# Joining the layer-2 experts, their combination and the layer-3 linear attention into one program per engine, with the keys computed in step with the queries

## The reference

```python
# layer 2, feed-forward: top 2 of 8 experts, then layer norm
h = gelu(einsum('bsd,edf->bsef', x, w1) + b1)
expert_out = einsum('bsef,efd->bsed', h, w2) + b2
out = einsum('bse,bsed->bsd', gate_probs, expert_out)      # 2 rows per token
out = (out - mean) / sqrt(var + 1e-5) * ln_g + ln_b
x = x + tanh(g_ffn[2]) * out
# layer 3, linear attention (8 heads of 64)
q = softmax(layer_norm(layernorm(x) @ Wq, ln_q_g, ln_q_b), -1) * 8
k, v = split(context @ Wkv); k, v = with a null key and value in front
k = softmax(k, over tokens)
ctx = einsum('bhnd,bhne->bhde', k, v)
out = layer_norm(einsum('bhnd,bhde->bhne', q, ctx)) @ Wout
x = x + tanh(g_xattn[3]) * out
# layer 3, feed-forward: top 2 of 8 experts with a capacity
```

## Time and profile before

| | |
|---|---|
| median of 3 runs | 1698.0 us (1695.79 to 1702.94) |
| the profiled execution | 1712.41 us, its span 1710.7 us |
| mean granted TensorE clock | 0.865 |
| busy over the span: PE, DVE, ACT, POOL | 71%, 58%, 40%, 47% |
| layer-2 experts, first weight load to last store | 831.0 to 1015.0 us |
| combination, first load to last instruction | 1023.7 to 1085.2 us |
| linear attention, first load to last scatter | 1085.9 to 1424.3 us |
| layer-3 experts and last combination | 1432.4 us to the end |

### The profile page before, as it was taken

The page is one execution under the profiler, slowest core; times in us unless marked ns, Lnnn a source line. Parts: engine busy times, 40 slices in busy tenths (PEclk is TensorE's granted clock), DMA queues, the critical chain, the costliest instruction groups (busy, mean ns, idle before and its releaser), DMA issues. The chain is left out here.

```text
span 1710.7 us, 36170 instructions
## 1 busy us (share of the span) xinstructions
PE 1217.5 (71%) x11764; PEld 981.9 (57%) x11764; DVE 992.1 (58%) x2935; ACT 691.6 (40%) x1614; POOL 812.3 (47%) x1064
## 2 busy tenths in 40 slices
PE   3888864918888697554489960388888853999991
PEld 2666653916676474344378850256666643888881
DVE  3877861247998575576122219678888841444444
ACT  2766641316887253442133320145555421222222
POOL 1347564517776135456344430145777762333334
PEclk9998976967999798775699985699999976999996
DMA  5322203633331002011466633100000002222215
GB/s 131 104 90 88 71 14 101 199 78 125 107 112 52 13 2 67 8 39 46 135 194 191 195 104 99 38 2 2 15 18 18 18 26 75 63 77 61 75 38 152
DMA packets 156107, 130.03 MB, mean 76 GB/s; under 512 B 21402, under 2 KB 133804, under 8 KB 155952
## 3 DMA queue, kind: packets, MB, share of 16 engines
q1 hardware_dynamic: 144688, 106.98, 22.0%
q0 software_dynamic: 11264, 21.07, 3.6%
...
## 5 line engine op out<-in xcount | busy, mean ns | idle before, releaser
L1324 POOL DMA_INDIRECT l_rows_out<-l3e_y,l3e_target x80 | 77.8, 973 | 176.0 <-DVE l3e_y L1311 163.8
L1278 ACT ACTIVATE l3e_sT<-l3e_ps_h 128x256 f32<-128x256 f32 x160 | 61.5, 384 | 177.9 <-PE l3e_ps_h L1248 151.5
L1324 POOL DMA_INDIRECT l_rows_out<-l2e_y,l2e_target x80 | 77.8, 972 | 115.0 <-DVE l2e_y L1309 97.2
L1297 DVE TENSOR_TENSOR l3e_hT<-l3e_sT,l3e_ps_h 128x256 f32<-128x256 f32 x160 | 67.4, 421 | 99.5 <-ACT l3e_sT L1278 97.9
L1275 ACT ACTIVATE l2e_hT<-l2e_ps_h,l2e_b 128x256 f32<-128x256 f32 x160 | 66.9, 474 | 111.5 <-PE l2e_ps_h L1243 101.7
L1247 PE MATMUL l3e_ps_h<-l3e_xT,l3e_w 128*128 128x256 f32 x320 | 101.0, 398 | 4.9 <-DVE l3e_xT L1288 0.6
L1248 PE MATMUL l3e_ps_h<-l3e_xT,l3e_w 128*128 128x256 f32 x320 | 96.6, 384 | 0.0
L1040 POOL DMA_INDIRECT l_rows_in<-l2a_rt_rows,l2f_slot x64 | 62.9, 982 | 61.0 <-DVE l2f_slot L1030 43.6
L1257 PE MATMUL l2e_ps_y<-l2e_w,l2e_hT 128*128 128x128 f32 x640 | 81.3, 281 | 1.0 <-issue 0.9
L1257 PEld LDWEIGHTS l2e_ps_y<-l2e_w,l2e_hT 128*128 128x128 f32 x640 | 77.0, 196 | 2.2 <-issue 1.8
L1243 PE MATMUL l2e_ps_h<-l2e_xT,l2e_w 128*128 128x256 f32 x320 | 77.6, 386 | 0.7 <-DVE l2e_xT L1288 0.6
...
## 6 DMA issues: line engine op xcount, KB each, us to landing
...
```

Of the source, the lines that this page charges most:

```text
L1278: nc.scalar.activation(sT[:, f % 2, :], ps_h[f % 2][:, 0:CHUNK], act_func).then_inc(s_ready, 1)
L1297: nc.vector.tensor_tensor(hT[:, b, f, :], sT[:, f % 2, :], ps_h[2 + f % 2][:, 0:CHUNK], ALU.mult).then_inc(h_ready, 1)
L1324: pool.indirect_dma_start(out=r.rows_out, out_offset=bass.IndirectOffsetOnAxis(ap=target[:, c % 2, a:a + 1], axis=0), in_=y[:, c % 2, a, : ...
```

## The change

The three phases become one, `experts_then_attention`: no barrier between them, and each engine runs the experts' part, then the linear attention's. `Combine` is no longer a phase; its parts stand inside the linear attention's steps, four tiles at a time, and are spread over ScalarE (weighting `scale`, normalising `normal`), GpSimd (`total`, `root`, `update`) and VectorE (moments, `offset`). The loop now begins at step -17 instead of -6. Since x is turned raw and not normalised, the layer norm in front of the queries goes into the weights (centred columns, `wqc`, `wq_total`) and into the variance (`x_eps_of`); ScalarE's L2226 and the shared `statistics` of the phase fall away. The null key's exponent is its own small ScalarE instruction instead of a VectorE addition (L2336). SyncE issues the gains and the attention's weights ahead of the experts' loads, and VectorE adds the shift to x ahead of the experts. KEY_LEAD = 0 and KEY_EARLY = 0 mean that the keys of tile i+3 stay in step i, as before. The diff, cut to its core:

```diff
+KEY_LEAD = 0
+KEY_EARLY = 0
...
+    def scale(self, act, t):
+        if not self.is_tile(t):
+            return
+        if t % 4 == 0:
+            act.wait_ge(self.arrived[t // 4], 32)
+        for k in (1, 0):
+            self.nc.scalar.activation(self.got[:, k, t, :], self.got[:, k, t, :], ACT.Copy, scale=self.r.weight[:, k, t:t + 1]
+                                      ).then_inc(self.s["scaled"], 1)
+
+    def total(self, pool, q):
+        if not self.is_quad(q):
+            return
+        at = slice(4 * q, 4 * q + 4)
+        pool.wait_ge(self.s["scaled"], 8 * q + 8)
...
+    def root(self, pool, q):
+        if not self.is_quad(q):
+            return
+        at, s = slice(4 * q, 4 * q + 4), self.s
+        pool.wait_ge(s["mom_ready"], 4 * q + 4)
+        pool.wait_ge(s["filled"], 1)
+        pool.tensor_scalar(self.veps[:, q % 2, :], self.moments[:, at, 1], LN_EPS, None, ALU.add).then_inc(s["veps_ready"], 1)
+        pool.wait_ge(s["veps_ready"], q + 1)
+        pool.tensor_tensor(self.rstd[:, at], self.veps[:, q % 2, :], self.half[:, :], ALU.pow).then_inc(s["root_ready"], 1)
+
+    def offset(self, dve, q):
+        if not self.is_quad(q):
+            return
+        at = slice(4 * q, 4 * q + 4)
+        dve.wait_ge(self.s["root_ready"], q + 1)
+        self.nc.vector.scalar_tensor_tensor(out=self.nmr[:, at], in0=self.moments[:, at, 0], scalar=-1.0, in1=self.rstd[:, at],
+                                            op0=ALU.mult, op1=ALU.mult).then_inc(self.s["nmr_ready"], 1)
...
+        act.wait_ge(self.s["nmr_ready"], t // 4 + 1)
+        self.nc.scalar.activation(self.got[:, 0, t, :], self.got[:, 0, t, :], ACT.Identity, scale=self.rstd[:, t:t + 1], bias=self.nmr[:, t:t + 1]
+                                  ).then_inc(self.s["normed"], 1)
...
+        at, s = slice(4 * q, 4 * q + 4), self.s
+        pool.wait_ge(s["gated"], 2)
+        pool.wait_ge(s["shifted"], 1)
+        pool.wait_ge(s["normed"], 4 * q + 4)
+        got = self.got[:, 0, at, :]
+        pool.tensor_tensor(got, got, self.lnp[:, 0, :].unsqueeze(1).broadcast_to([P, 4, D]), ALU.mult).then_inc(s["gained"], 1)
+        pool.wait_ge(s["gained"], q + 1)
+        pool.tensor_tensor(self.core.x[:, at, :], self.core.x[:, at, :], got, ALU.add).then_inc(s["added"], 1)
...
+            pool.wait_ge(s["xnT_ps"], t + 1)
+            pool.wait_ge(s["qsq_ready"], t + 1)
+            pool.wait_ge(before.s["xbn_ready"], t + 1)
+            pool.tensor_tensor(core.x[:, t, :], core.x[:, t, :], shift[:, :], ALU.add).then_inc(s["x_shifted"], 1)
...
+        for i in range(FIRST, NT + 9):
+            query_centred(i + 2)
+            key_norm(key_tile(i) - 2)
+            router.prefix(pool, quad(i - 5))
+            router.scatter_tile(pool, i - 9)
+            roots(i)
+            before.update(pool, quad(i + 9))
+            shifted(i + 3)
+            null_values(key_tile(i))
+            router.roots_on_pool(pool, quad(i - 1))
+            before.root(pool, quad(i + 13))
+            before.total(pool, quad(i + 17))
+        router.scattered(pool)
...
+            pe.wait_ge(before.s["added"], t // 4 + 1)
+            reused(pe, s["qb_ready"], t - 1)
+            nc.tensor.transpose(ps_x, core.x[:, t, :], core.ident[:, :]).then_inc(s["xnT_ps"], 1)
...
+        for i in range(FIRST, NT + 9):
+            k = key_tile(i)
+            turned_keys(k - 1)
+            query_exponents(i + 1)
+            before.normal(act, i + 9)
+            turned_outputs(i - 1)
+            key_exponents(k)
+            turned_queries(i + 1)
+            values(k)
+            before.scale(act, i + 17)
+            turned_x(i + 5)
+            router.turned(act, quad(i - 3), ps_t)
+            router.normalise(act, quad(i - 2))
...
+        for i in range(FIRST, NT + 9):
+            k = key_tile(i)
+            query_maximum(i + 2)
+            before.offset(dve, quad(i + 12))
+            query_squares(i + 4)
+            query_denominators(i)
+            query_variance(i + 4)
+            outputs(i)
+            key_maximum(k)
+            output_moments(i)
+            key_centred(k)
+            output_mean(i)
+            query_offset(i + 3)
+            output_variance(i)
+            combined(k - 1)
+            before.row_moments(dve, i + 13)
+            residual(i - 1)
+            before.x_moments_of(dve, i + 5)
+            before.row_mean(dve, i + 13)
+            router.read(dve, quad(i - 4), ps_l)
+            router.slots(dve, quad(i - 5), ps_l)
+            key_denominators(k - 1)
+            before.x_mean_of(dve, i + 5)
+            summed(i - 1)
+            before.x_eps_of(dve, i + 5)
+            router.choose(dve, quad(i - 4))
+            router.aggregate(dve, i - 1, s["summed"])
+            router.offsets(dve, quad(i - 2))
+        router.gaps(dve)
+        router.weights(dve, 1e-12, route_gate)
+    return Programs(sync, tensor, scalar, vector, gpsimd), prepare
...
+            combine.load_gains(sp)
+            attention.sync(sp)
+            expert.sync(sp)
+            all_stored(sp)
+            combine.load_rows(sp)
...
+            expert.tensor(pe)
+            psum_free(pe)
+            attention.tensor(pe)
...
+            combine.shift(dve)
+            expert.vector(dve)
+            attention.vector(dve)
...
+            combine.prepare(pool)
+            prepare(pool)
+            expert.gpsimd(pool)
+            attention.gpsimd(pool)
...
```

1501 lines of the change are left out of this document (772 added, 729 removed).

## The result

The changed kernel takes 1692.78 us in the median of 20 runs (1681.43 to 1700.41), the kernel before 1700.7 (20 runs, 1689.39 to 1707.9). The ratio is 0.9953 with a 95% interval of 0.9933 to 0.9974. Two repetitions on other chips gave 0.9944 (0.9921 to 0.9968) and 0.9944 (0.9915 to 0.9972). So the gain is 8 to 9.5 us, where I forecast 19 (1679). Two single executions in a slow state, 1785.46 us of the kernel before and 3100.58 us of `warm_start`, are left out of all ratios.

What follows compares the result with a forecast made beforehand. VectorE bounds the combination, PE's chain plain attention steps, VectorE choice steps. -51 + 2.5 + 12 + 1.6 + 16 = -19, from the runs' median of 1698.0 to 1679 us; range 1657 to 1696.

Steps and rivals of the forecast that it cites:

- The start, -51: Start of the attention: first copy of the turned x (`xnT`) at 1050 instead of 1101.3 us.
- The experts' delay: Ahead of the experts: issuing gains and attention's weights first makes the experts start 7.2 us later.
- mostly the landing of the stores; I keep it: Last expert store to first row load: 9.7 us kept; the missing barrier may take off some tenths.
- Load to first `xnT`: First row load to first copy of the turned x: 1030.2 to 1050 us.
- The weightings, +12: Steps -5 to 14: ScalarE's two weightings between `v` and `xnT` lengthen each by 0.61 us; bounds 0 and 16.
- The new wait, +16: Every fourth step: VectorE's `offset` waits for GpSimd's inverse root, 16 us in sum; bounds 0 and 25.
- VectorE, +1.6: Loop: some 0.7 us more VectorE work per step, hidden in plain steps, counting 1.6 us in choice steps.
- the holds: VectorE operations held by GpSimd on shared ports: 12 us either way, up to 32 if uncovered; none booked.
- The cold clock, +2.5: First three loop steps: TensorE's clock is low after some 20 us of idle; 2.5 us, bounds 0 and 5.
- Rival 2: Loop steps -3 to 26: GpSimd becomes the bound and holds VectorE, so slower, 1715 us; chance 0.09.
- Rival 3: No change, 1694 us: stores land later or loads crowd the experts, and the wait costs 25; chance 0.14.
- its upper 25 us for the wait: The wait of `offset` at its upper bound, 25 us, if centred queries or key norms are late too.

Runs made afterwards that it cites:

- warm_start: Changed kernel with 56 unread products of the identity with itself on PE behind the attention's preamble: ratio 0.9979 to the kernel before.
- both: Changed kernel with the root one step earlier and ScalarE's two weightings behind the copy of the turned x: 1677.82 us, ratio 0.9766 to the kernel before.
- both_form: Changed kernel with the root one step earlier, the weightings behind the turned x's copy, and query_variance as tensor_scalar: ratio 0.9738 to the kernel before.
- form: Changed kernel with VectorE's query_variance as tensor_scalar instead of scalar_tensor_tensor: ratio 0.9939 to the kernel before.
- warm: Changed kernel with 18 unread identity products on PE in each of the six steps that hold an offset: ratio 0.9991 to the kernel before.

## Why the prediction was half right

The forecast was -19, and -8 to -9.5 was measured. By the second pair of profiles, with the forecast's terms laid on the stretches in which they fall:

```
us                                           forecast   measured
start, up to the first xnT                    -51        -54.0
first four steps of the loop                   +5.9       +4.4   (+2.8 and +8.5 in the other profiles)
five steps with an offset (3, 7, ..., 19)     +17.4      +24.5   (wait 15.0, weightings 2.4)
the other 22 steps                             +7.7      +13.1   (weightings 6.1, VectorE 1.6)
ahead of layer 2's attention, behind the loop   0         +4.0, +1.2
```

Another 1.2 of the forecast's weightings fall ahead of the first `nmk`.

- **The start, -51: right in sum, in part by luck.** The experts' delay was 7.6 (7.2 forecast). "mostly the landing of the stores; I keep it" was wrong: 7.5 of the 9.7 us went with the barrier, where I had allowed some tenths. Load to first `xnT` gained 53.9 where I forecast 57. The first error is worth 6.8 us, the second takes 3.1 of them back, the experts 1.1 more; so the sum comes near for no good reason.
- **The weightings, +12: right, a little high.** Plain steps went from 7.99 to 8.56, and moving the pair gave back 9.4 us.
- **The new wait, +16: right in place and mechanism, too low.** `nmk` to `nmk` was 13.8 against 12.2; the five steps with an offset grew by 24.5 us where the forecast has 17.4, and a step of lead took 19.8 of them back and 23 us of the time. The 1.07 us by which `offset` is held in each are some 5 of the 7.1 us missed: it runs directly behind the root, when GpSimd has just started its next wide operation, and that stood in GpSimd's order. The sum has 0.15 for it.
- **VectorE, +1.6, with the holds booked at nothing: the step that failed.** The prediction names the mechanism and prices it at up to 32 us, then says "the wait of plain steps covers most" and "I book none of it". That holds for plain steps and not where VectorE has no wait to hide in. With the wait and the weightings both gone (`both`), the loop is still 12.4 us longer than before, with about 6 us more at half clock (11.0 against 5.3). It stands in the steps beside the choices: 21.8, 21.8 and 20.3 instead of 18.1 us for the three pairs, and 2.0 us in step 24. There the added moments that I had counted cost no more than the removed L2336 gives back (0.32 against 0.28), and the 2.0 us are held operations (1.26) and the wait for GpSimd's key norm (0.70). The changed form of `query_variance`, which I had taken for "a small scalar operation", costs 0.47 us more in the mean (588 against 116 ns), and `offset` up to 1.96 us in place of 0.15. Without the first (`both_form`) the pairs are still 20.8, 20.8 and 19.6. What the holds cost in time is not shown by themselves: `form` took the first away and the kernel was no faster.
- **The cold clock, +2.5: open.** In the first profile of the changed kernel the clock was 0.95 in the first four steps, as good as before the change (0.94), and they cost 2.8 us more, hardly more than their four weightings; in the third it was 0.72 and they cost 8.5. Over the loop the time at half speed rose from 5 to 43 to 76 us, and in the changed kernel's own profiles a longer loop goes with more of it (305 with 42.7, 315 with 75.6). `warm` cut it to 18.6 and gained nothing measurable, with its products in the way. What share of the 42 to 52 us is the clock's stays open.
- Together: -54 + 42 to 52 and about +1 at the end is -11 to -1 us by the profiles, around the measured 8 to 9.

Rival 2 saw the mechanism, VectorE held by GpSimd and late key norms, but put it in every step and the total at slower. It acts where VectorE is the bound, around the choices and behind each wait. Rival 3 came nearest in time, 1694 against 1692.78, and its upper 25 us for the wait is close to the 24.5 of the five steps; its other half, that the stores land later with no barrier or the loads cost more than 7.2 us, hardly came true (2.2 us and 7.6).
